# Second cross attention of a decoder block: scores as three fp32r products, and one buffer instead of two for the attended values

## What is computed

```python
q = (hidden_states @ Wq.T).reshape(bsz, q_len, 32, 128).transpose(0, 2, 1, 3)
k = (cross_attention_states @ Wk.T).reshape(bsz, kv_len, 8, 128).transpose(0, 2, 1, 3)
v = (cross_attention_states @ Wv.T).reshape(bsz, kv_len, 8, 128).transpose(0, 2, 1, 3)
q = _rmsnorm(q, q_norm_w)
k = _rmsnorm(jnp.repeat(k, 4, axis=1), k_norm_w)
v = jnp.repeat(v, 4, axis=1)
scores = jnp.einsum('bhqd,bhkd->bhqk', q, k) / np.sqrt(128) + attention_mask
out = jnp.einsum('bhqk,bhkd->bhqd', softmax(scores), v)
return out.transpose(0, 2, 1, 3).reshape(bsz, q_len, 32 * 128) @ Wo.T
```

## Time and profile before

| | us |
|---|---|
| median of three executions (1640.35 to 1643.02) | 1641.4 |
| the profiled execution | 1641.55 |
| its span, first to last instruction | 1639.8 |
| outside the span | 1.75 |
| TensorE busy | 1551.3 (95%) |
| VectorE busy | 946.8 (58%) |
| ScalarE busy | 799.7 (49%) |
| GpSimd busy | 768.3 (47%) |

### The profile page before, as it was taken

One profiled execution on the slowest core, in us unless ns is written; L12 is line 12 of the kernel. 1 busy time (PEld: TensorE's weight loads), 2 busy tenths in 40 slices (PEclk: granted clock), 3 DMA queues, 4 the chain that ended last, 5 costly groups with the idle time before them and its releaser, 6 DMA issues. The chain is left out here.

```text
span 1639.8 us, 29510 instructions
## 1 busy us (share of the span) xinstructions
PE 1551.3 (95%) x10984; PEld 1289.0 (79%) x10984; DVE 946.8 (58%) x1685; ACT 799.7 (49%) x2426; POOL 768.3 (47%) x623
## 2 busy tenths in 40 slices
PE   6899999999998899998999889999999999999997
PEld 4777897888886578776777678888888888888875
DVE  3847502332366688778667735555555555555756
ACT  3352324444443555536888735544554454455432
POOL 3413214444322798844433536655555545555413
PEclk9999999999999899999999999999999999999998
DMA  6100200000120452204000021201101101100001
GB/s 212 39 1 1 58 20 21 21 21 22 53 87 18 167 180 90 91 1 123 1 2 27 27 92 39 66 28 38 52 14 53 39 27 39 34 27 14 1 1 52
DMA packets 61777, 77.84 MB, mean 47 GB/s; under 512 B 12168, under 2 KB 41348, under 8 KB 61636
## 3 DMA queue, kind: packets, MB, share of 16 engines
q1 hardware_dynamic: 61172, 74.63, 14.3%
q0 software_dynamic: 464, 1.32, 0.3%
HBM read 73.85 MB, written 2.10 MB: 46 GB/s over the span
## 5 line engine op out<-in xcount | busy, mean ns | idle before, releaser
L1198 POOL TENSOR_TENSOR xa_rs<-xa_ms,minus_half 128x5 f32<-128x5 f32 x64 | 74.7, 1168 | 159.4 <-DVE xa_ms L1469 159.3
L1204 POOL TENSOR_TENSOR xa_prob<-xa_prob,xa_inv 128x512 f32<-128x512 f32 x64 | 66.7, 1042 | 139.0 <-DVE xa_inv L1436 139.0
L789 POOL TENSOR_TENSOR xa_prob<-xa_prob,xa_inv 128x1024 f32<-128x1024 f32 x32 | 60.6, 1895 | 140.8 <-DVE xa_inv L1067 140.8
L1464 DVE TENSOR_REDUCE xa_ssq<-pre 128x4 f32<-128x512 f32 x64 | 43.9, 686 | 133.2 <-ACT pre L1400 133.2
L1414 ACT ACTIVATE xa_prob<-xa_prob,xa_peak 128x128 f32<-128x128 f32 x256 | 99.7, 391 | 41.9 <-DVE xa_peak L1480 41.9
L1803 DVE SCALAR_TENSOR_TENSOR ff_acc<-ff_ring,ff_sT,ff_acc 128x512 f32<-128x512 f32 x140 | 100.2, 747 | 30.7 <-ACT ff_acc L1756 17.8
L108 PE MATMUL late_bank<-late_q_hi,xT_hi 128*128 128x512 f32 x284 | 117.5, 414 | 0.0
L110 PE MATMUL late_bank<-late_q_lo,xT_hi 128*128 128x512 f32 x284 | 112.2, 395 | 0.0
L109 PE MATMUL late_bank<-late_q_hi,xT_lo 128*128 128x512 f32 x284 | 112.1, 395 | 0.0
L1400 ACT ACTIVATE pre<-late_bank 128x512 f32<-128x512 f32 x64 | 38.2, 597 | 140.2 <-PE late_bank L110 140.2
L2040 POOL TENSOR_TENSOR pre<-pre,sa_inv 128x1024 f32<-128x1024 f32 x32 | 63.7, 1989 | 91.2 <-DVE sa_inv L2247 91.2
(11 more groups left out here) (434 smaller groups left out, 4967.9 us busy)
## 6 DMA issues: line engine op xcount, KB each, us to landing
pre<-in_wq SPq DMA_DIRECT2D x8, 1024.0 KB, 5.6
late_raw_o<-in_wo SPq DMA_DIRECT2D x8, 1024.0 KB, 5.4
pre<-in_wq SPq DMA_DIRECT2D x16, 192.0 KB, 3.2
pre<-in_wo SPq DMA_DIRECT2D x16, 192.0 KB, 4.0
ff_dn_q<-in_down_w SPq DMA_DIRECT2D x6, 512.0 KB, 3.8
ff_dn_z<-in_down_z SPq DMA_DIRECT2D x6, 512.0 KB, 5.2
ff_dn_s<-in_down_s SPq DMA_DIRECT2D x6, 512.0 KB, 5.9
pre<-in_xT SPq DMA_DIRECT2D x4, 512.0 KB, 8.0
```

The lines of the kernel that those rows point to most:

```text
L789: pool.tensor_tensor(prob[:, t % 3, :, :], prob[:, t % 3, :, :], bc(inv[:, t % 3, :], 2, [P, Q, KEYS]), ALU.mult).then_inc(s["norm"], 1)
L1198: pool.tensor_tensor(rs[:, :], ms[:, :], m.minus_half[:, 0:Q + 1], ALU.pow).then_inc(s["rs"], 1)
L1204: pool.tensor_tensor(prob[:, u % 2, :, :], prob[:, u % 2, :, :], bc(inv[:, u % 2, :], 2, [P, Q, S]), ALU.mult).then_inc(s["norm"], 1)
```

## The change

The turned queries and keys are no longer copied as plain fp32. ScalarE writes their high parts, VectorE two new low parts at the head of its step, and the scores are made by `three`. `scores` and `turn_qk` now wait for the low parts. `out_hi` and `out_lo` have one buffer each, so their writes wait for the output projection of the unit just before.

```diff
-        qT = sb("qT", [P, Q, S])
+        qT_hi, qT_lo = (sb(n, [P, Q, S], F32R) for n in ("qT_hi", "qT_lo"))
+        kT_hi, kT_lo = (sb(n, [P, S], F32R) for n in ("kT_hi", "kT_lo"))
...
-        out_hi, out_lo = (sb(n, [P, 2, Q, S], F32R) for n in ("out_hi", "out_lo"))
+        out_hi, out_lo = (sb(n, [P, Q, S], F32R) for n in ("out_hi", "out_lo"))
...
                 def scores(u):
-                    pe.wait_ge(s["qT"], u + 1)
+                    pe.wait_ge(s["kT_lo"], u + 1)
+                    pe.wait_ge(s["qT_lo"], u + 1)
                     if u:
                         pe.wait_ge(s["masked"], u)
                     for h in range(Q):
-                        last = pe.matmul(score[:, h * P:(h + 1) * P], qT[:, h, :], kT[:, :], start=True, stop=True)
+                        last = three(pe, score[:, h * P:(h + 1) * P], qT_hi[:, h, :], qT_lo[:, h, :], kT_hi[:, :], kT_lo[:, :], True, True)
...
-                        act.activation(kT[:, :], kt[:, 0:P], ACT.Copy, scale=nw2[:, :]).then_inc(s["kT"], 1)
-                        act.activation(qT[:, :, :].rearrange("p h n -> p (h n)"), qt[:, :], ACT.Copy).then_inc(s["qT"], 1)
+                        act.activation(kT_hi[:, :], kt[:, 0:P], ACT.Copy, scale=nw2[:, :]).then_inc(s["kT"], 1)
+                        act.activation(qT_hi[:, :, :].rearrange("p h n -> p (h n)"), qt[:, :], ACT.Copy).then_inc(s["qT"], 1)
...
                         act.wait_ge(s["pv"], u + 1)
-                        if u >= 2:
-                            act.wait_ge(s["rows"], u - 1)
+                        if u:
+                            act.wait_ge(s["rows"], u)
...
                 for t in range(STEPS):
+                    u = t - 1
+                    if 0 <= u < UNITS:
+                        dve.wait_ge(s["kT"], u + 1)
+                        if u:
+                            dve.wait_ge(s["score"], u)
+                        dve.scalar_tensor_tensor(kT_lo[:, :], kt[:, 0:P], nw2[:, :], raw(kT_hi[:, :]), ALU.mult, ALU.subtract).then_inc(s["kT_lo"], 1)
+                        dve.wait_ge(s["qT"], u + 1)
+                        dve.tensor_tensor(qT_lo[:, :, :].rearrange("p h n -> p (h n)"), qt[:, :],
+                                          raw(qT_hi[:, :, :]).rearrange("p h n -> p (h n)"), ALU.subtract).then_inc(s["qT_lo"], 1)
                     u = t - 2
                     if 0 <= u < UNITS:
                         dve.wait_ge(s["exp"], u + 1)
...
                         dve.wait_ge(s["out_hi"], u + 1)
-                        if u >= 2:
-                            dve.wait_ge(s["rows"], u - 1)
+                        if u:
+                            dve.wait_ge(s["rows"], u)
```

More of the change, by code:

```diff
@@ L1106, in cross1_stage @@
         qn = m.pre[:, KC * D:KC * D + Q * HD].rearrange("p (h n) -> p h n", h=Q)
-        kn, kT, mask = (m.pre[:, KC * D + Q * HD + n * P:KC * D + Q * HD + (n + 1) * P] for n in range(3))
-        qT = sb("qT", [P, Q, S])
+        kn, mask = (m.pre[:, KC * D + Q * HD + n * P:KC * D + Q * HD + (n + 1) * P] for n in range(2))
+        qT_hi, qT_lo = (sb(n, [P, Q, S], F32R) for n in ("qT_hi", "qT_lo"))
+        kT_hi, kT_lo = (sb(n, [P, S], F32R) for n in ("kT_hi", "kT_lo"))
         v_hi, v_lo = (sb(n, [P, 3, HD], F32R) for n in ("v_hi", "v_lo"))
@@ L1117, in cross1_stage @@
             "ld_q", "ld_kv", "ld_o", "ld_c", "kv0_hi", "q0_hi", "kv0_lo", "q0_lo", "hi", "split_q", "split_kv", "split_o",
-            "nw", "kv_mm", "q_mm", "ksq", "v", "v_lo", "sq", "ssq", "ms", "rs", "qn", "kn", "qk_turn", "kT", "qT", "score", "masked",
+            "nw", "kv_mm", "q_mm", "ksq", "v", "v_lo", "sq", "ssq", "ms", "rs", "qn", "kn", "qk_turn", "kT", "qT", "kT_lo", "qT_lo", "score", "masked",
             "peak", "exp", "inv", "norm", "turn", "prT", "pr_lo", "pv", "out_hi", "out_lo", "rows", "add")}
@@ L1266, in turn_qk @@
                     if u:
-                        pe.wait_ge(s["qT"], u)
+                        pe.wait_ge(s["kT_lo"], u)
+                        pe.wait_ge(s["qT_lo"], u)
                     if u - 4 >= UNITS - B:
@@ L1306, in out_rows @@
                     for h in range(Q):
-                        last = three(pe, rows[:, :], out_hi[:, u % 2, h, :], out_lo[:, u % 2, h, :],
+                        last = three(pe, rows[:, :], out_hi[:, h, :], out_lo[:, h, :],
                                      o_hi[:, g % 2, h, :], o_lo[:, g % 2, h, :], h == 0, h == Q - 1)
@@ L1314, in turn_batch @@
                     if u == UNITS - B:
-                        pe.wait_ge(s["kT"], u + 4)
+                        pe.wait_ge(s["kT_lo"], u + 4)
                     else:
-                        pe.wait_ge(s["kT"], min(u + 4, UNITS))
+                        pe.wait_ge(s["kT_lo"], min(u + 4, UNITS))
                         pe.wait_ge(n4["lo"], u - (UNITS - B))
@@ L1359, in _ @@
                 values(UNITS - 1)
-                base(2, "qT", UNITS)
+                base(2, "qT_lo", UNITS)
                 out_rows(UNITS - 1)
@@ L1406, in _ @@
                         act.wait_ge(s["pv"], u + 1)
-                        if u >= 2:
-                            act.wait_ge(s["rows"], u - 1)
-                        act.activation(out_hi[:, u % 2, :, :].rearrange("p h n -> p (h n)"), mixed[:, :], ACT.Copy).then_inc(s["out_hi"], 1)
+                        if u:
+                            act.wait_ge(s["rows"], u)
+                        act.activation(out_hi[:, :, :].rearrange("p h n -> p (h n)"), mixed[:, :], ACT.Copy).then_inc(s["out_hi"], 1)
                     u = t - 1
@@ L1494, in _ @@
                         dve.wait_ge(s["out_hi"], u + 1)
-                        if u >= 2:
-                            dve.wait_ge(s["rows"], u - 1)
-                        dve.tensor_tensor(out_lo[:, u % 2, :, :].rearrange("p h n -> p (h n)"), mixed[:, :],
-                                          raw(out_hi[:, u % 2, :, :]).rearrange("p h n -> p (h n)"), ALU.subtract).then_inc(s["out_lo"], 1)
+                        if u:
+                            dve.wait_ge(s["rows"], u)
+                        dve.tensor_tensor(out_lo[:, :, :].rearrange("p h n -> p (h n)"), mixed[:, :],
+                                          raw(out_hi[:, :, :]).rearrange("p h n -> p (h n)"), ALU.subtract).then_inc(s["out_lo"], 1)
 INNER = 1792
```

## The result

The changed kernel takes 1982.66 us in the median of five runs (1971.76 to 1986.71), the kernel before 1641.0 beside it: a ratio of 1.2075, 95% interval 1.2055 to 1.2094, so 342 us slower. The forecast was 1960, in a range of 1860 to 2050. The profiled execution is the quickest of the five, with a mean granted clock of 0.921; the other four have 0.914 to 0.916.

A forecast was written before the change was run, and what follows sets the result against it. TensorE, busy 95% of the span, was taken as the bound. Stalls 199.5, scores 29.4, step 2 and the last scores 4.0 and clock 85.4 made 318 us on 1641.55, so 1960 us, range 1860 to 2050.

The forecast's parts named there:

- The scores: TensorE's score block: 12 fp32r products of 128 columns at 0.114 us, 1.36 us, 0.46 more a unit.
- Columns alone: Rival on TensorE's scores: 128-column fp32r products cost 0.059 us each, 42 us less, 1918 us; chance 0.09.
- a whole fp32 product: Rival on TensorE's scores: each fp32r product costs 0.225 us, 86 us more, 2046 us; chance 0.11.
- the 81 ns: Skill page's issue gap for score products: 12 take 0.97 us, about 1935 us; chance counted within a rival of 0.09.
- The chain: From the output projection's end through ScalarE, VectorE and GpSimd to `turned`: 4.97 us, TensorE stalls 3.27 us a step.
- 1874 in the sum: Rival: TensorE's clock stays up despite the stalls, 1641.5 + 233 = 1874 us; chance 0.12.
- One chain of two edits: Single out buffer and VectorE's low parts both delay the reciprocals: stall 3.27 us together, 1.77 from VectorE's order alone.
- The slack of 0.20: Before the change, softmax weights leave GpSimd 0.20 us before TensorE loads for `turned`.
- The clock: TensorE falls to half clock in nearly every step, 3.4 us long, costing 1.4 us: 61 x 1.4 = 85.4 us.
- a rival of 0.06: Half-clock stretch on TensorE lasts twice as long, 104 us more, 2064 us; chance 0.06.
- forecast 1781: Rival: only one of the two delays bites, stall 1.77 us, 1781 us, up to 1865 with clock loss; chance 0.05.
- The tail: Behind the loop, the last scores wait for the low part of the queries: 2.2 us more.

The follow-up runs named there:

- the run of the products alone: Kernel before, scores as three fp32r products of high parts only, no low parts, one buffer for the probabilities: 1667.66 us, ratio 1.0159.
- with the clock held: Changed kernel with 12 idle fp32 products in front of the turning of the softmax weights: 1866.01 us, ratio 1.1376.
- one buffer: Kernel before with single out_hi and out_lo, scores in plain fp32 and no low parts: 1756.69 us, ratio 1.0704.
- VectorE's order alone: Changed kernel with two buffers for out_hi again and one for the probabilities, low parts still ahead of the reciprocals: 1771.55 us, ratio 1.0802.
- the same kernel without a stall: Kernel before (step 9.59 us), or changed kernel with two out_hi buffers and reciprocals, then out_lo, ahead of the low parts (step 10.03 us, 1672.64 us).
- those with one delay: Changed kernel with two out_hi buffers and one for the probabilities, 1771.55 us; changed kernel with reciprocals moved ahead of the low parts, 1787.27 us.
- a gap of 2.1 us: Changed kernel with 4 idle fp32 products in front of the turning of the softmax weights: 1892.75 us, ratio 1.1529.
- gaps of 1.65 and 1.46 us: Changed kernel with one edit undone: reciprocals moved ahead of the low parts (1787.27 us), or two out_hi buffers and one for the probabilities (1771.55 us).

## Why the prediction was right

**The scores.** Forecast 1.36 us for 12 products, 0.46 more a unit; the step grew by 0.43. In the profile after, the score products of one head start 0.11 us apart:

```profile
1118.33 0.28 PE L108 MATMUL late_bank<-xa_kT_hi,xa_qT_hi 128*128 128x128 f32 x1
1118.44 0.28 PE L109 MATMUL late_bank<-xa_kT_hi,xa_qT_lo 128*128 128x128 f32 x1
1118.56 0.27 PE L110 MATMUL late_bank<-xa_kT_lo,xa_qT_hi 128*128 128x128 f32 x1
1118.67 0.27 PE L108 MATMUL late_bank<-xa_kT_hi,xa_qT_hi 128*128 128x128 f32 x1
```

It is the price of a transpose with the same 128 columns and of a record of the fp32 product. Columns alone (0.059) and a whole fp32 product (0.225) are both refuted, by this and by the run of the products alone. With the 107 ns a load of the Trainium skill (TensorE: Matmul & The Clock Gate, LDWEIGHTS) the trace agrees to 5 ns (0.1115 us, the mean of ten spacings in this step); the 81 ns of the same page's Back-to-back issue gap it does not bear out.

**The chain.** Forecast 4.97 us from the end of the projection to the load, a gap of 3.1 us and a step of 13.32 at full clock. Measured: 4.94 us from 1109.82 to 1114.76, where the load starts too; a gap of 2.99; a step of 13.23. From there to the end of the next projection are 8.28 us, forecast 8.35. Nothing else joined: with the clock held, the whole kernel took 1866.0, against 1874 in the sum.

**One chain of two edits.** Forecast stalls of 1.90 (one buffer), 1.77 (order) and 3.27 us (both). Held against the same kernel without a stall, the steps give 11.46 - 9.59 = 1.87, 11.70 - 10.03 = 1.67, and 13.23 - 10.03 = 3.20. So both together cost 0.34 less than the sum of 3.54. The prediction's rows give the reason. With VectorE's order alone, the copies of the turned keys and queries start 0.58 us behind the projection's end (1101.55 to 1102.13), when TensorE has turned them; with both edits they start at 1111.95, 2.13 behind it, and that turning has long been done beside `out_hi` and the exponentials. The slack of 0.20, which is used up only once, counts the other way: 0.58 - 0.20 = 0.38. All of this could be worked out from the rows of before, since both edits put something late in front of the same instruction, the reciprocals, in the lists of two engines.

**The clock.** The mechanism was right and its size was off. Forecast was a fall in every step worth 1.4 us, 85 us in all, and 104 at most; it cost 117 (1982.7 against 1866.0). The term that was too small was the length of the stretch: I took 3.4 us at half clock each time, from the earlier trace rows, and held 6.8 for a rival of 0.06. A single stretch of 3.4 us was worth what I took: a step with one is 14.5 to 14.8 us, 1.3 to 1.6 over 13.23. In the locked pattern the two lengths alternate, and a step with 6.8 us is 15.9, 2.7 over; two steps take 30.7 us where 2 x 13.23 are 26.5, so 2.1 us a step. Why the longer ones come was not tested. Up to about 1160 us only 5 of 12 steps were hit in the profiled run (the clock is at 0.97 from 1060 to 1140 us), which brought its mean below that; the other four executions, at a lower mean clock, have no trace here:

```profile
1060.00:1140.00 80.00, 63.32 (x358) 54.08 (x357) 37.21 (x77) 26.93 (x96) 29.77 (x27) 0.97 0.07 21
```

The forecast was only 23 us low because two errors partly cancelled: the clock cost 31 us more than the 85, and the rest was 8 too high. The rivals stood at the right places: the run without the falls took 1866 (forecast 1874), those with one delay 1772 and 1787 (forecast 1781).

**The tail.** Forecast 2.2 us for the last scores. From the last `turn_qk` to the next stage are 39.28 us after against 33.74 before, 5.5 more. The wait itself came as forecast. Before, the last scores started 1.65 us after the last `turn_qk` (1573.79); after, they start 3.95 after it (1898.46), 2.3 later. Of before:

```profile
1575.44 0.38 PE L1280 MATMUL late_bank<-pre,xa_qT 128*128 128x128 f32 x1 [0.94 <-ACT xa_qT L1380]
```

Of after, and the stretch behind that gap:

```profile
1902.41 0.44 PE L108 MATMUL late_bank<-xa_kT_hi,xa_qT_hi 128*128 128x128 f32 x1 [3.24 <-DVE xa_kT_lo L1439]
```

```profile
1901.72:1908.55 6.83, 6.14 (x21) 5.40 (x22) 2.82 (x7) 0.00 (x0) 1.60 (x2) 0.50 0.00 0
```

What the prediction left out here is the clock, which it charged to the steps of the loop alone. Behind this gap of 3.24 us, too, it was at 0.50 for 6.8 us. The 12 score products took 0.4 us more than the 8 records, and the remaining 2.8 of the 5.5 fall into that stretch.

## What to carry to other kernels

Put nothing late in front of an instruction that another engine's next wait leads to: here two small instructions on an engine at half load, and one wait that "only" moved from two units back to one, cost 310 us, and the same instructions in another order cost none of it. When a buffer is taken away, look at what stands behind its writer in that engine's list, not at the writer. And when TensorE is to stall by some microseconds in each step, count the clock as well: filling the gap with idle products brought back 117 us here, and removing the stall 310.

## What the hardware showed that I had not expected

The clock's falls lock to the steps. With a gap of 2.98 us in each step they settle into 6.8 and 3.4 us at half clock in turn, and stay so for 23 pairs; with a gap of 2.1 us one comes every two to four steps; with gaps of 1.65 and 1.46 us the stretches of 1000 to 1600 us have 1.00. Near the end of the stage, in each of the two profiled runs with gaps of 1.65 us, one gap is 1.9 us long, and a stretch of 3.4 us at 0.50 stands behind it (at 1645 and 1666 us). So the 2.05 us gap of the earlier trace rows, after which the clock stayed, marks no safe length. At half clock the spacing of 512-column fp32r products is 0.43 us (from 0.233). The four transposes in front of them are slowed as well:

```profile
1168.94 1.12 PE L1291 MATMUL xa_turn<-ident,xa_prob 128*128 128x128 f32 x4 [2.98 <-POOL xa_prob L1205]
1169.71 0.78 PE L108 MATMUL late_bank<-late_q_hi,xT_hi 128*128 128x512 f32 x1
...
1170.71 0.63 PE L110 MATMUL late_bank<-late_q_lo,xT_hi 128*128 128x512 f32 x1
1171.13 0.63 PE L108 MATMUL late_bank<-late_q_hi,xT_hi 128*128 128x512 f32 x1
```

They take 0.77 us to the next product's start, against 0.41 at full clock in the step shown first (1114.76 to 1115.17). What the chip looks at before it lets the clock fall was not tested, and the runs do not tell it.
